# The involution's shift of the logits moved from VectorE to GpSimd, between its feature differences; the exponentials of four rows of taps asked for later

## The reference, cut to what matters

```
x1 = conv1x1(x, w1, b1); x2 = conv1x1(x, w2, b2); x3 = conv1x1(x, w3, b3)
sub2 = x1[:, :, None] - unfold_patches(x2)          # 7*7 = 49 neighbours
feat = concatenate([sub2, subp], axis=1)            # subp: the same of positions
y = relu(bn1(feat)); y = conv1x1(y, cw1)
y = relu(bn2(y));    wgt = conv1x1(y, cw2, cb2)     # 49 logits per pixel
wgt = softmax(wgt, axis=2)                          # over the 49 neighbours
out = sum over the 49 taps of patch(x3) * wgt[tap]
```

## Time and profile before

| | |
|---|---|
| time, median of 3 runs | 4944.77 us (4943.57 to 4947.01) |
| the profiled execution | 4947.29 us, span 4945.5 us |
| PE busy | 4412.9 us (89%) |
| DVE busy | 3706.2 us (75%) |
| ACT busy | 1972.1 us (40%) |
| POOL busy | 480.9 us (10%) |
| products, line 622 | 686, 2137 ns each |
| feature differences, line 456, POOL | 98, 4539 ns each |
| shifts, line 582, DVE | 98, 2157 ns each |

### The profile page before, as it was taken

How to read it: one execution, slowest core, us unless ns; L and a number is a source line. 1 busy time by engine, 2 the same in 40 slices (tenths; PEclk the granted TensorE clock), 3 DMA queues, 4 the chain that set the end, 5 groups by cost and what they waited for, 6 DMA issues and landing times. The chain is left out here.

```text
span 4945.5 us, 69464 instructions
## 1 busy us (share of the span) xinstructions
PE 4412.9 (89%) x26634; PEld 2616.1 (53%) x26634; DVE 3706.2 (75%) x3410; ACT 1972.1 (40%) x3026; POOL 480.9 (10%) x188
## 2 busy tenths in 40 slices
PE   5789999999999999997698888979888879999999
PEld 2267767777677777777334343343343324444544
DVE  6189888898888898888656676575674637787877
ACT  1443433434333434331364544646536433332321
POOL 1231112211212212110000000000000000000000
PEclk9899999999999999999899999999999989999999
DMA  6300100010100101000201101110110010000000
GB/s 204 112 28 31 35 28 25 25 35 31 35 27 15 35 31 35 28 10 30 73 1 54 46 21 47 45 28 21 57 43 20 12 60 23 30 26 26 30 26 23
DMA packets 88752, 186.90 MB, mean 38 GB/s; under 512 B 14622, under 2 KB 78158, under 8 KB 85378
## 3 DMA queue, kind: packets, MB, share of 16 engines
q1 hardware_dynamic: 86274, 177.51, 11.4%
q0 software_dynamic: 1744, 4.89, 0.3%
q10 hardware_dynamic: 432, 0.20, 0.0%
HBM read 103.60 MB, written 59.70 MB: 33 GB/s over the span
## 5 line engine op out<-in xcount | busy, mean ns | idle before, releaser
L622 DVE TENSOR_TENSOR prod<-lg,win 128x1792 f32<-128x1792 f32 x686 | 1430.3, 2137 | 6.3 <-PE ps L690 5.5
L690 PE MATMUL ps<-ident,prod 128*128 128x128 f32 x9604 | 1196.4, 277 | 148.9 <-DVE prod L622 127.5
L690 PEld LDWEIGHTS ps<-ident,prod 128*128 128x128 f32 x9604 | 1097.0, 143 | 306.6 <-DVE prod L622 160.3
L456 POOL TENSOR_TENSOR y<-a1w,x2w 128x1568 f32<-128x1568 f32 x98 | 444.8, 4539 | 1560.2 <-PE ps L668 1542.0
L535 ACT ACTIVATE y<-ps,u2c,s2c 128x392 f32<-128x392 f32 x392 | 265.7, 678 | 787.2 <-PE ps L668 787.2
L1066 ACT ACTIVATE phq<-ps 128x896 f32<-128x896 f32 x448 | 384.4, 917 | 202.2 <-PE ps L1327 200.7
L1162 DVE TENSOR_TENSOR phk<-kv 128x2048 f32<-128x2048 f32 (+1 forms) x200 | 455.7, 2281 | 0.4
L675 PE MATMUL ps<-y,cw2bd 128*128 128x392 f32 x784 | 362.3, 544 | 0.8 <-ACT lg L542 0.8
L1699 PE MATMUL ps<-xn,w_s 128*128 128x448 f32 x896 | 352.6, 548 | 6.2 <-ACT hid L1536 6.2
L667 PE MATMUL ps<-y,cw1bd 128*128 128x392 f32 x784 | 327.7, 500 | 31.0 <-ACT y L528 25.5
L1718 PE MATMUL ps<-hid,w_s 128*128 128x448 f32 x896 | 347.7, 542 | 0.6 <-DVE ybuf L1627 0.6
(11 more groups left out here) (211 smaller groups left out, 4736.1 us busy)
## 6 DMA issues: line engine op xcount, KB each, us to landing
win<-planes SPq DMA_DIRECT2D x14, 2480.0 KB, 8.7
qst<-qsp SPq DMA_DIRECT2D x96, 196.0 KB, 4.6
planes<-stage SPq DMA_DIRECT2D x7, 1984.0 KB, 7.0
xs<-in_x SPq DMA_DIRECT2D x8, 1568.0 KB, 21.1
conv_dram<-osb SPq DMA_DIRECT2D x14, 896.0 KB, 4.5
t<-in_x SPq DMA_DIRECT2D x28, 448.0 KB, 4.0
xn<-conv_dram SPq DMA_DIRECT2D x28, 448.0 KB, 8.0
t_dram<-tout SPq DMA_DIRECT2D x28, 448.0 KB, 2.9
```

What stands on the lines that cost most here:

```text
L456: pool.tensor_tensor(o, x1, x2, ALU.subtract).then_inc(z_ready, 1)
L622: v.tensor_tensor(prod[b.buf(t)][:].rearrange("p (s h w) -> p s h w", h=RW, w=W), w, xw, ALU.mult).then_inc(prod_ready, 1)
L690: mm = pe.matmul(acc[:, at:at + P], data, ident[:], start=(t == 0 and k % 4 == 0), stop=(t == NU - 1), is_transpose=True, skip_group_check ...
```

## The change

The shift leaves DVE's queue and enters POOL's. In each slot POOL now does: difference 0 of block a, shift 3 of block b, difference 1, shift 4, difference 2, shift 5, difference 3, shift 6, differences 4 to 6, and then, waiting for the fold of block a, shifts 0, 1 and 2 of block a. The exponentials of rows of taps 3 to 6 move on ACT from units 1, 3, 6 and 9 to units 7, 12, 17 and 23; those of rows 0 to 2 stay. DVE's fold gets one more wait: it may not overwrite `mx` before the previous block's seven shifts are done.

```
-SHIFT_NEXT = {1: 3, 3: 4, 6: 5, 9: 6}
+SHIFT_NEXT = {7: 3, 12: 4, 17: 5, 23: 6}
+SHIFT_FIRST, SHIFT_LATER = 3, {0: (3,), 1: (4,), 2: (5,), 3: (6,)}
...
         @block.gpsimd
...
+            def shift(b, i):
+                pool.wait_ge(maxed, 5 * (b.n + 1))
+                l = lg[b.par][:, i]
+                pool.tensor_tensor(l, l, mx[:].unsqueeze(1).broadcast_to([P, K7, PW]), ALU.subtract).then_inc(shifted, 1)
+
             def slot(a, b):
+                for i in range(K7):
+                    if a:
+                        z(a, i)
+                    if b and i in SHIFT_LATER:
+                        for k in SHIFT_LATER[i]:
+                            shift(b, k)
                 if a:
-                    for i in range(K7):
-                        z(a, i)
+                    for k in range(SHIFT_FIRST):
+                        shift(a, k)
...
         @block.vector
...
-            def shift(b, i):
-                v.wait_ge(maxed, 5 * (b.n + 1))
-                l = lg[b.par][:, i]
-                v.tensor_tensor(l, l, mx[:].unsqueeze(1).broadcast_to([P, K7, PW]), ALU.subtract).then_inc(shifted, 1)
...
                     v.wait_ge(maxed, m + 3)
+                    if b:
+                        v.wait_ge(shifted, K7 * a.n)
                     v.tensor_tensor(mx[:], half[:, 0], half[:, 2], ALU.max).then_inc(maxed, 2)
...
-                    if a and u in SHIFT_NOW:
-                        shift(a, SHIFT_NOW[u])
-                    if b and u in SHIFT_NEXT:
-                        shift(b, SHIFT_NEXT[u])
```

## The result

The changed kernel takes 5186.05 us (5181.66 to 5189.05, 4 runs) against 4944.17: 242 us more, a ratio of 1.0487 with a 95% interval of 1.0469 to 1.0506. The forecast was 5108, the range 5035 to 5170. The direction was right, the size too small by a third, and the time lies outside the range.

What follows compares the result with a forecast made beforehand. PE and DVE are near full; only DVE's work in the turn, or later starving of PE, sets the time. 12 turns x 12 = 144, first turn 10, last 9.5: 163.5 more, about 5108 us; range 5035 to 5170.

Steps and rivals of the forecast that it cites:

- The turn: From the fold to PE's unit 2: about 36 us instead of 24; taken as 12 us lost in each of 12 turns.
- the first of my three: In the turn, POOL gets in after each DVE product: 5.0 us a pair, unit 2 at T+36.8, 12.8 us late.
- the three orders: In the turn, POOL gets in after every product, three times in four, or once DVE stops; all end 12 to 13 late.
- The step that failed: Around units 6 and 12, difference-shift pairs stall DVE 6.1 us each; hidden by PE's pace, 1 to 3 us if buffers aren't full.
- My own sign of a wrong forecast: The forecast is wrong if, among other signs, the loss arises past unit 6.
- Gain from removal: Four shifts leaving DVE in the turn save 1.70 us each, 6.8 a slot; units 3, 6, 9 nothing except last slot.
- First and last turn: The turn after block 0 loses 10 us; the turn into the last, DVE-bound slot loses 9.5.
- Other parts: Later exponentials on ACT and the fold's new wait cost nothing; SP's loads are unchanged.
- Faster: Rival: POOL's shifts don't hold DVE up; 95 us less, 4850, if the stall is under 1.0 us; chance 0.05.
- More: Rival: low clock at the chunk and starved buffers; 17 us a turn, 228 in all, 5173; chance 0.14.
- starved buffers around units 6 to 16: Part of the rival of 5173 us (chance 0.14): buffers run short around units 6 to 16.
- the low clock at unit 2: If unit 2 with its chunk begins at 1.2 GHz, 4.0 us become 8, 4 more; set at 0 in the sum.

Runs made afterwards that it cites:

- shifts 5 and 6 later: The changed kernel with shifts 5 and 6 on POOL behind differences 4 and 5 instead of 2 and 3, exponentials at units 24 and 30: 5155 us.
- the run with POOL in the middle: Against the kernel before: shifts 3 to 6 on POOL behind differences 2 to 5, exponentials at units 13, 19, 24 and 30; shifts 0 to 2 stay on DVE: 5030 us.
- nine small operations: The kernel before with nine extra small DVE multiplications a slot, beside units 3 to 7, 13 to 15 and 19, result unused: 4990 us.
- the run with idle transposes: The changed kernel with differences 0 and 1 ahead of the fold, plus 14 idle PE transposes behind each of units 44 to 48: 5140 us.

## Why the prediction was wrong, step by step

- **The turn.** "Unit 2 is ready at 15.5 + 7 x 3.05 = T+36.8": measured 38.3. The order was the first of my three, strictly one POOL operation to one product, in all 13 turns. The 1.5 us are the shift's stall, 3.31 instead of 3.05. I had taken the difference's length for it. My first order gave 12.8 us for the turn and I took 12, a mean over the orders; measured 14.3 in the slot shown and 13.8 in the mean. Which of the three orders would come, the prediction had left open.
- **The step that failed.** "Difference 2 is followed by shift 5, difference 3 by shift 6: each pair stalls DVE 6.1 us in some 10, while PE uses three of four buffered products; hidden, barely". In the first of my three orders, the one that came, this stood at nothing. DVE did refill after the turn, as I wrote (a lead of 8.3 us at unit 7). But at the reciprocal it waits for the old block's sums, and at unit 9 the lead was 3.1 us, about one unit of PE and not four. The pairs used it up: PE waited at units 10 and 15, and from unit 7 to the last logit a slot lost 3.1 us. With shifts 3 to 6 back on DVE it lost nothing there, with shifts 5 and 6 later 0.7. My own sign of a wrong forecast, a loss "past unit 6", came true.
- **The sizes.** 12 x (17.7 - 12) = 69 us were missing in the full slots: about 22 in the turn (13.8 against 12), 37 behind unit 7, and 8 between units 2 and 7, where unit 2 ran at 1.2 GHz in five of the 12 turns (1.6 us each), which I had also set at nothing. Counting DVE's time alone, 7 x (3.31-1.70) + 2 x 3.09 = 17.5 a slot, comes as near to the measured 17.7, but such a count supposes that DVE's waits stay what they were, and in the run with POOL in the middle they didn't.
- **Gain from removal**, 6.8 us a slot, and nothing for the shifts of units 3, 6 and 9: 6.0 in the turn shown without any shift, 4.2 in the mean of 12 turns, and nothing behind it. The step was right, its size too large.
- **First and last turn**, 10 and 9.5: 14.8 (13.2 with its earlier fold) and 11.3. The last is the under-count of the stall, 7 x (3.31-1.70) = 11.3.
- **Other parts.** Exponentials, SP and the fold's new wait: nothing, as said.
- **Rivals.** "Faster" needed a stall under 1.0 us and fell with the shift's 3.31. "More" gave 17 a slot and 5173, nearest to the truth, and named both things that I left out of the sum: "starved buffers around units 6 to 16", which came to 3.1 us a slot, and the low clock at unit 2, which came in five turns of 12 and cost 1.6 us and not 4. It had 0.14. The clock isn't what makes the turn's 14.3: unit 2 starts when its product is there, at T+38.3, in nearly all turns.

The Trainium skill, "GPSIMD Engine Reference", section 3.1, gives 4497 ns for such an operation of 2048 elements; scaled to 1568 that is an estimate of 3.44 us. This case's trace is a little below it: 3.24 us for a difference beside an idle DVE, and 3.31 for what a shift takes from DVE.

## What to carry to other kernels

Before work is added to an engine because its consumer is the bound, read how far it is ahead of that consumer at each step, from the end of its output to the consumer's start, and don't count on full buffers. Here PE never waited between unit 2 and the last logit, yet the lead was 0.4 us at one unit and 6.3 ten units later, and a wait of the producer itself (the reciprocal's) kept it from growing. A time that comes out as expected doesn't prove the mechanism: nine small operations cost a slot just what they add up to, but by way of a POOL operation that they kept waiting for 20 us. When an elementwise operation with two inputs in SBUF moves from VectorE to GpSimd beside VectorE operations of the same kind, count what VectorE loses while it is held (here 3.31 us) against what it saves (1.70); unless these fall into its waits, the move costs. Moving work on the same engine out of the stretch that sets the time (here three of the four shifts in the turn) gave 38 us with two lines.

## What the runs showed of the hardware

- A POOL subtraction of 128 x 1568 in place with a broadcast operand held DVE for 3.31 us, one with a strided, overlapping operand 3.09.
- A POOL operation that began right behind another got in after one DVE product at most (never over 5.33 us in any run, five or seven in a row in the turns). One that POOL began out of idleness often did too, but could also wait for as long as DVE started operation after operation: 16.79 us at 280.52 in the kernel before, 20.4 us in every full slot of the run with more DVE work early.
- PE in a rhythm of one unit each 5.24 us mostly alternated between 1.2 and 2.4 GHz from unit to unit (3.2 and 1.75 us, granted clock 0.52 and 1.00), with some units in between.
- At the jump of its loop PE waited 4.48 us once in the run without a shift, and 4.71 to 5.48 us five times in the run with idle transposes, for nothing that the profile shows.
